# Attention on one core: another order of widths, decay sums, scores and chunk ends on TensorE

## The chip, the cores and the metric

The kernel runs on one core of a Trainium2 chip. The metric is the device time of one execution in microseconds (us); lower is better. The core has TensorE (PE, matrix products; PEld is its weight load), VectorE (DVE), ScalarE (ACT), GpSimd (POOL) and SyncE (SP, which issues transfers). Each works through its own instructions in the order in which they are written; semaphores tie the engines together.

## The reference

A block of a gated transformer on x of 32 batches x 512 rows x 512 columns: an mLSTM-like attention with 8 heads of 64 columns (queries from x, keys and values from a context), then a layer of experts, each row's choice of experts by a softmax. The attention part, cut to what matters:

```
gi = concat([q, k, v]);  ig = gi @ igate_w.T + igate_b;  fg = gi @ fgate_w.T + fgate_b
cs = cumsum(log_sigmoid(fg));  log_D = tril(cs_s - cs_t) + ig_t
D = exp(log_D - max(log_D));  C = (q @ k.T / sqrt(64)) * D
h = (C / (max(abs(C.sum(-1)), exp(-max_log_D)) + 1e-6)) @ v
x = x + tanh(g_xattn) * layernorm_per_head(h) * out_w
```

Then x = x + tanh(g_ffn) * experts(layernorm(x)).

## The kernel before

Two stages follow each other: `attention`, in a loop over batches, then `experts`, eight experts with four blocks of rows each. Only the first is touched.

**Attention, chunk by chunk.** A batch has 512 rows, cut into four chunks of 128 (TILES). Inside a chunk the products of queries and keys are formed and weighted with the decays; what lies before a chunk comes in by a running state. The eight heads go in four pairs (PAIRS), p = 0 to 3. For each pair TensorE has four steps: `decays(b, p)` sums the logarithms of the decays into the bank EX (10 products; ScalarE's `decay_factors` takes the exponential into C); `widths(b, p)` spreads a factor of each row over the columns of its heads (one product; VectorE's `weighted_queries` multiplies the queries with it); `scores(b, p)` is the product of queries and keys into the two banks QK (16 products; VectorE's `weighted_scores` multiplies them with C); `product(b, p)` applies the result to the values and the states, into A (ScalarE's `numerators` copies it out).

**The loop.** It has NB + 2 = 34 iterations i, and holds five batches at a time: b1 = i - 1 (its q and k are transposed and its gates worked out), b2 = i - 2 (the four pairs), b3 (end of pair 3, normalising), b5 = i - 5 (`turn_rows`, the transposes of its finished rows xfb for the router, and `logits`) and b6. `live(b)` says whether there is such a batch. Each engine's order in the loop is written out by hand.

**Gates.** For b1, `gates` (TensorE) sums the gate logits, `log_sigmoid` (ScalarE) takes their logarithms, `shift_gates` (TensorE) moves rows into the bank T1, `gate_runs` (VectorE) makes the running sums and `rise` out of it. `chunk_ends` (TensorE, two small products into T0) hands the ends of the chunks over to `gate_peaks` (VectorE), which copies them into `prior` and goes on to `peaks`. VectorE's order there is gate_runs(b1), weighted_queries(b2, 3), gate_peaks(b1), weighted_scores(b2, 3), inner_factors(b1) (which ends with `steps`). `peaks` is needed by decays(b1, 0), and `steps` by `turn_gates` (TensorE) at the end of the iteration.

**Banks.** T[0], T[1] and the two QK banks are shared by many short-lived products. The table in `iteration_fills` says which product goes to which of the four (the last number of an entry) and which engine empties it; `fill` makes TensorE wait until the bank's last content has been taken. By that table widths of pair 1 go to T0 and those of pairs 2 and 3 to T1. T1 holds the copy of q (column block 3) ahead of widths of pair 2, and the product of `shift_gates` ahead of widths of pair 3:

```
                    ("qw", b2, 2, "dve", 1), ("scores", b2, 2, None, None), ("shift", b1, 0, "dve", 1), ("qw", b2, 3, "dve", 1),
```

The first two `turn_rows` of b5 also go to T1 one after the other, and ScalarE empties them in `turned_rows`. ScalarE's order there is: copies of q and k (blocks 0 and 1 of b1), first_state(b2), second_norm(b5, (2, 3)) (which finishes xfb), squares(b3, 3), decay_factors(b2, 1), turned_rows(b5, 0), turned_rows(b5, 1). `scores` of pair 1 waits until VectorE has taken the states (S) out of the two QK banks.

Of the kernel before, what the change touches and what calls it, by code (L numbers as in the profile page):

```python
# [75 lines left out]
def spread(ap, axis, n):  # L76

    ap = ap.unsqueeze(axis)
    return ap.to_broadcast([n if i == axis else s for i, s in enumerate(ap.shape)])
# [9 lines left out]
def attention(nc, io, NB, dram, sm_all, tg, consts, stored, plan):  # L89
# [6 lines left out]
    with ExitStack() as ctx:  # L96
# [60 lines left out]
        def live(b):  # L157
            return 0 <= b < NB
# [36 lines left out]
        def fill(pe, kind, b, k):  # L195

            if ahead[kind, b, k]:
                pe.wait_ge(*ahead[kind, b, k])
            if (kind, b, k) in weighted:
                pe.wait_ge(*weighted[kind, b, k])  # L200
            return bank[kind, b, k]
# [46 lines left out]
        with nc.Block() as block:  # L248
# [410 lines left out]
            def _(pe):  # L659
# [8 lines left out]
                def turn(kind, b, c):  # L668

                    src, blocks = (q, None) if kind == "q" else (kraw, b % VBUF)  # L670
                    t = fill(pe, kind, b, c)
                    for j in range(TILES):
                        rows = q[:, j, :] if kind == "q" else kraw[:, b % VBUF, j, :]
                        mm = pe.transpose(t[:, j * P:(j + 1) * P], rows[:, c * P:(c + 1) * P], ident[:, :])
                    mm.then_inc(s["tfull"], 1)
# [62 lines left out]
                def scores(b, p):  # L738

                    g = PAIRS * b + p  # L740
                    if g:
                        pe.wait_ge(s["cc"], 2 * g)
                    for taken in cleared.get((b, p), ()):
                        pe.wait_ge(*taken)
                    for j in range(TILES):
                        jj = slice(j * P, (j + 1) * P)
                        for par in range(2):
                            r = slice(DH * par, DH * par + DH)
                            mm = pe.matmul(QK[:, par, jj], kT[r, b % 2, p, jj], qT[r, b % 2, p, jj], start=True, stop=True)  # L749
                    mm.then_inc(s["qk"], 1)  # L750

                def decays(b, p):

                    g = PAIRS * b + p
                    if g:
                        pe.wait_ge(s["dd"], g)
                    top, end = slice(0, DH), slice(DH, P)
                    for a, r, mask in ((0, top, (maskneg, maskswap)), (1, end, (maskswap, maskneg))):
                        for t, m in zip((top, end), mask):
                            pe.matmul(EX[t, a, :], identb[r, r], m[r, :], start=True, stop=False, skip_group_check=True)  # L760
                    if p == 0:
                        pe.wait_ge(s["rp"], b + 1)
                    for a, r in ((0, top), (1, end)):
                        ones_of = pick[r, p, :, :].rearrange("k a j -> k (a j)")
                        pe.matmul(EX[:, a, :], climb[r, b % 2, :], spread(ones_of, 2, P), start=False, stop=False, skip_group_check=True)
                    if p == 0:
                        pe.wait_ge(s["xm"], b + 1)
                    for par in range(2):
                        for a, r in ((0, top), (1, end)):
                            half = slice(a * 2 * P, (a + 1) * 2 * P)  # L770
                            mm = pe.matmul(EX[:, a, par * 2 * P:(par + 1) * 2 * P], sel[r, 2 * p + par, :], peaks[r, b % 2, half],
                                           start=False, stop=True, skip_group_check=True)
                            if par:
                                mm.then_inc(s["ee"], 1)

                def widths(b, p):

                    t = fill(pe, "qw", b, p)
                    pe.matmul(t[:, 0:SEQ - P], selP[:, 2 * p:2 * p + 2, :].rearrange("k a d -> k (a d)"), inner[:, b % 2, :], start=True, stop=True)\
                      .then_inc(s["tfull"], 1)  # L780
# [11 lines left out]
                def product(b, p):  # L792

                    g = PAIRS * b + p
                    pe.wait_ge(s["cc"], 2 * g + 2)
                    if p == 0:
                        wait_taken(pe, "st", b, TILES - 2)
                    wait_taken(pe, "qw", b, p)
                    if g:
                        pe.wait_ge(s["an"], g)  # L800
                    for j in range(TILES):
                        for par in range(2):
                            for a in range(2):
                                r = slice(DH * a, DH * a + DH)
                                mm = pe.matmul(A[r, par, j, 0:VW], C[:, 2 * (g % CRING) + par, j * P + DH * a:j * P + DH * a + DH],
                                               vc[:, b % 2, j, 2 * p + par, :], start=(j == 0), stop=(j == 0), skip_group_check=True)
                    for j in range(1, TILES):
                        for par in range(2):
                            r = slice(DH * par, DH * par + DH)
                            mm = pe.matmul(A[:, par, j, 0:VW], qw[r, g % 2, (j - 1) * P:j * P], S[r, j - 1, p, :],  # L810
                                           start=False, stop=True, skip_group_check=True)
                    mm.then_inc(s["af"], 1)

                for i in range(NB + 2):
                    b1, b2, b3, b5, b6 = i - 1, i - 2, i - 3, i - 5, i - 6

                    if live(b3):
                        product(b3, 3)
                    if live(b2):
                        widths(b2, 0)  # L820
                    if live(b1):
                        pe.wait_ge(s["q"], b1 + 1)
                        pe.wait_ge(s_cd[b1 % VBUF], 16 * (b1 // VBUF + 1))
                        for c in range(2):
                            turn("q", b1, c)
                            turn("k", b1, c)
                    if live(b2):
                        for j in range(TILES - 1):
                            chunk_state(b2, j)

                        decays(b2, 1)
                    if live(b5):
                        turn_rows(b5, 0)
                    if live(b2):
                        widths(b2, 1)
                        scores(b2, 1)
                    if live(b5):
                        turn_rows(b5, 1)
                    if live(b2):
                        product(b2, 0)  # L840
                    if live(b5):
                        turn_rows(b5, 2)
                    if live(b1):
                        turn("q", b1, 2)
                        turn("k", b1, 2)
                        turn("q", b1, 3)
                    if live(b6):
                        turn_logits(b6)
                    if live(b5):
                        turn_rows(b5, 3)  # L850
                    if live(b1):
                        turn("k", b1, 3)

                    if live(b2):
                        decays(b2, 2)
                        widths(b2, 2)
                        scores(b2, 2)
                    if live(b1):
                        gates(b1)
                    if live(b2):  # L860
                        product(b2, 1)
                    if live(b1):
                        if b1 == 0:
                            pe.wait_ge(s["prep1"], 1)
                        shift_gates(b1)

                    if live(b2):
                        decays(b2, 3)
                        widths(b2, 3)
                    if live(b1):  # L870
                        chunk_ends(b1)
                    if live(b2):
                        scores(b2, 3)
                    if live(b5):
                        logits(b5)
                    if live(b2):
                        product(b2, 2)
                    if live(b1):
                        decays(b1, 0)
                        scores(b1, 0)  # L880
                        turn_gates(b1)
# [971 lines left out]
```

## Time and profile before

| | us |
|---|---|
| median of 3 runs | 3052.46 |
| lowest, highest | 3051.99, 3055.52 |
| span of the profiled execution (first to last instruction) | 3051.6 |
| TensorE busy in it | 2948.7 (97%) |
| VectorE busy | 1819.7 (60%) |
| ScalarE busy | 1132.8 (37%) |
| GpSimd busy | 1065.5 (35%) |

The profiled execution's own time shown is its span; the median of the runs lies 0.9 us above it. The shares are means over two unlike stages: VectorE and ScalarE are far busier in attention than over the span. Instructions on TensorE are pipelined, so that one starts before the one ahead of it is over; where steps are added up, the distance from start to start is taken.

### The profile page before, as it was taken

What the parts mean: (1) busy time and instruction counts of PE and PEld (TensorE: products, weight loads), DVE (VectorE), ACT (ScalarE), POOL (GpSimd) and SP (SyncE); (2) the same over time, 40 slices, a digit from 0 to 9 for tenths busy, and PEclk for the clock granted to TensorE, in tenths of its full rate; (3) what the DMA queues carried; (4) which work ended last, traced back from release to release, by engine and by line L of the source; (5) the groups of instructions that cost most, each with busy time, mean ns of one, the idle gap of its engine ahead of it and who ended that gap; (6) DMA issues with size and microseconds to landing.
All of it is one profiled execution on the core that took longest, in us unless ns stands there. A gap on an engine that the chain in (4) does not pass through costs nothing.

```text
span 3051.6 us, 60802 instructions
## 1 busy us (share of the span) xinstructions
PE 2948.7 (97%) x24708; PEld 2395.3 (78%) x24708; DVE 1819.7 (60%) x5124; ACT 1132.8 (37%) x2025; POOL 1065.5 (35%) x1029
## 2 busy tenths in 40 slices
PE   6999999999997599999999999999999999999998
PEld 5888888888886477777777877787787787778886
DVE  6999999999998645354454444444434445444332
ACT  5788788787886211121121121122112122112110
POOL 4777777777776311111122111121112112121111
PEclk9999999999998699999999999999999999999999
DMA  3243444434443412241242132232123214222121
GB/s 122 100 160 120 162 139 149 161 123 165 141 134 113 131 40 37 35 99 31 46 99 48 36 80 35 37 96 62 31 38 93 41 31 111 38 50 57 35 37 24
DMA packets 140575, 250.71 MB, mean 82 GB/s; under 512 B 31968, under 2 KB 31968, under 8 KB 140296
## 3 DMA queue, kind: packets, MB, share of 16 engines
q1 hardware_dynamic: 106296, 170.80, 17.2%
q0 software_dynamic: 28672, 67.65, 12.6%
q10 hardware_dynamic: 5328, 8.36, 0.9%
q8 instruction: 197, 3.23, 0.4%
q14 instruction: 82, 0.67, 0.1%
HBM read 137.23 MB, written 101.19 MB: 78 GB/s over the span
## 4 chain that ended last, share of the span: by engine, by line
PE 64%; DVE 1%; DMA 1%; issue 0%; ACT 0%; POOL 0%; ACTq 0%; DVEq 0%; POOLq 0%
PE DN L1729 32%; PE UP L1700 30%; PE TT L1673 1%; DMA w_raw<-in_L_ffn_W_down 1%; DVE c_hit L1392 0%; PE c_bank L1385 0%; DVE down_lo L1258 0%; PE c_bank L1369 0%; DVE c_hit L1413 0%; ACT z L1643 0%; DVE c_within L1408 0%; ACT down_hi L1252 0%; POOL out_x L1618 0%; DVE c_gained L1445 0%; DVE mid_lo L1761 0%
## 5 line engine op out<-in xcount | busy, mean ns | idle before, releaser
L1618 POOL DMA_INDIRECT out_x<-y,slots x128 | 208.5, 1629 | 1621.1 <-DVE y L1785 1621.1
L1643 ACT ACTIVATE z<-UP,bup 128x512 f32<-128x512 f32 (+1 forms) x352 | 240.8, 686 | 1085.6 <-PE UP L1700 1066.5
L1729 PE MATMUL DN<-down_hi,mid_hi 128*128 128x512 f32 x1408 | 570.8, 405 | 0.0
L1700 PE MATMUL UP<-xT_hi,up_lo 128*128 128x512 f32 (+1 forms) x1408 | 555.5, 395 | 0.0
L1700 PE MATMUL UP<-xT_hi,up_hi 128*128 128x512 f32 (+1 forms) x1408 | 553.5, 393 | 1.8 <-DVE xT_lo L1740 0.9
L1700 PE MATMUL UP<-xT_lo,up_hi 128*128 128x512 f32 (+1 forms) x1408 | 552.0, 392 | 0.0
L1729 PE MATMUL DN<-down_hi,mid_lo 128*128 128x512 f32 x1280 | 505.8, 395 | 0.0
L1729 PE MATMUL DN<-down_lo,mid_hi 128*128 128x512 f32 x1280 | 505.7, 395 | 0.0
L1759 DVE CAST mid_hi<-z 128x512 fp32r<-128x512 f32 (+1 forms) x352 | 151.2, 429 | 486.4 <-ACT z L1643 486.4
L1783 DVE TENSOR_TENSOR y<-DN,bdn 128x512 f32<-128x512 f32 x128 | 88.5, 692 | 432.3 <-PE DN L1729 419.5
L1700 PEld LDWEIGHTS UP<-xT_hi,up_hi 128*128 128x128 f32 (+1 forms) x1408 | 260.3, 185 | 67.5 <-ACT z L1643 2.8
L1700 PEld LDWEIGHTS UP<-xT_lo,up_hi 128*128 128x128 f32 (+1 forms) x1408 | 259.8, 185 | 67.6 <-issue 0.5
L1700 PEld LDWEIGHTS UP<-xT_hi,up_lo 128*128 128x128 f32 (+1 forms) x1408 | 259.9, 185 | 65.5 <-issue 0.5
L1729 PEld LDWEIGHTS DN<-down_hi,mid_hi 128*128 128x128 f32 x1408 | 266.5, 189 | 56.1
L1729 PEld LDWEIGHTS DN<-down_hi,mid_lo 128*128 128x128 f32 x1280 | 240.4, 188 | 58.2
L1729 PEld LDWEIGHTS DN<-down_lo,mid_hi 128*128 128x128 f32 x1280 | 241.1, 188 | 50.1
L1761 DVE TENSOR_TENSOR mid_lo<-z,mid_hi 128x512 fp32r<-128x512 f32 (+1 forms) x352 | 244.1, 693 | 12.1
L1627 ACT ACTIVATE xT_hi<-TT 128x512 fp32r<-128x512 f32 x126 | 68.3, 596 | 467.0 <-PE TT L1673 446.9
L233 POOL TENSOR_TENSOR nsb<-nsb,rr 128x512 f32<-128x512 f32 x125 | 127.0, 1049 | 215.2 <-DVE nn L973 215.2
L1030 DVE SCALAR_TENSOR_TENSOR C<-QK,C 128x512 f32<-128x512 f32 x256 | 164.7, 685 | 8.5 <-PE QK L749 6.5
L749 PE MATMUL QK<-qT,kT 64*128 64x128 f32 x2048 | 146.4, 282 | 13.2 <-DVE S L1048 12.1
L1597 POOL DMA_INDIRECT xg<-rows_scratch,slots x128 | 137.5, 1075 | 56.3 <-issue 38.1
(264 smaller groups left out, 4971.9 us busy)
## 6 DMA issues: line engine op xcount, KB each, us to landing
xs<-in_x SPq DMA_DIRECT2D x64, 512.0 KB, 3.7
kraw<-in_ctx SPq DMA_DIRECT2D x32, 1024.0 KB, 7.3
out_x<-xs SPq DMA_DIRECT2D x32, 1024.0 KB, 12.5
rows_scratch<-xfb SPq DMA_DIRECT2D x32, 1024.0 KB, 10.6
w_raw<-in_L_ffn_W_down SPq DMA_DIRECT2D x40, 512.0 KB, 4.4
w_raw<-in_L_ffn_W_up SPq DMA_DIRECT2D x16, 682.5 KB, 4.1
mid_hi<-mid_hi ACTq DMA_DIRECT2D x32, 86.0 KB
mid_lo<-mid_hi ACTq DMA_DIRECT2D x32, 84.0 KB
```

The costliest lines, as they stand in the source:

```text
L233: ins = eng.tensor_tensor(n, n, spread(scale[:, j, :], 2, DH), ALU.mult)
L749: mm = pe.matmul(QK[:, par, jj], kT[r, b % 2, p, jj], qT[r, b % 2, p, jj], start=True, stop=True)
L1030: dve.scalar_tensor_tensor(out=c, in0=QK[:, par, :], scalar=DH ** -0.5, in1=c, op0=ALU.mult, op1=ALU.mult)\
L1597: pool.indirect_dma_start(xg[:, t, :], None, rows_v, bass.IndirectOffsetOnAxis(ap=slots[:, 4 * n + t:4 * n + t + 1], axis=0)).then_inc(s_r ...
L1618: pool.indirect_dma_start(out_rows, bass.IndirectOffsetOnAxis(ap=slots[:, m:m + 1], axis=0), y[:, t, :], None, compute_op=ALU.add).then_in ...
L1627: act.activation(xT[0][:, c, :], turned(n, c)[:, :], ACT.Copy).then_inc(s["thi"], 1)
L1643: act.activation(z[0:r, k % 2, :], UP[k % 3][0:r, :], ACT.Silu, bias=bup[0:r, e // 2, f:f + 1]).then_inc(s["z"], 1)
L1700: mm = pe.matmul(UP[k % 3][0:r, :], weights.up[wa][:, c, f * P:f * P + r], xT[xa][:, c, :], start=first, stop=(c == CH - 1 and wa == 1))
L1729: mm = pe.matmul(DN[m % 2][:, :], lhs, rhs, start=first, stop=(f == FCH - 1 and lhs is parts[-1][0]))
L1759: dve.tensor_copy(mid[0][0:r, f, :], z[0:r, k % 2, :]).then_inc(s["hi"], 1)
L1761: dve.tensor_tensor(mid[1][0:r, f, :], z[0:r, k % 2, :], mid[0][0:r, f, :].bitcast(FP32), ALU.subtract)\
L1783: dve.tensor_tensor(y[:, t, :], DN[m % 2][:, :], bdn[:, e % 2, :], ALU.add).then_inc(s["yp"], 1)
```

## The change

Only the order of calls in TensorE's loop changes; every product stays, with the same operands, banks and waits. In pair 1, `decays` moves from ahead of `turn_rows(b5, 0)` and `widths` to behind them, directly ahead of `scores`. In pair 2, `widths` and `decays` change places. In pair 3 they change places too, and `scores` follows `decays` directly; `chunk_ends(b1)`, which stood ahead of `scores`, comes behind. The other engines' orders stay as they are.

```
                         for j in range(TILES - 1):
                             chunk_state(b2, j)
 
-                        decays(b2, 1)
                     if live(b5):
                         turn_rows(b5, 0)
                     if live(b2):
                         widths(b2, 1)
+                        decays(b2, 1)
                         scores(b2, 1)
...
                     if live(b2):
+                        widths(b2, 2)
                         decays(b2, 2)
-                        widths(b2, 2)
                         scores(b2, 2)
...
                     if live(b2):
+                        widths(b2, 3)
                         decays(b2, 3)
-                        widths(b2, 3)
+                        scores(b2, 3)
                     if live(b1):
                         chunk_ends(b1)
-                    if live(b2):
-                        scores(b2, 3)
```

TensorE's order at pair 1, before, from behind the states' products to the scores. EX takes the decay sums, T1 the transposed rows (from xfb), T0 the widths (from inner), QK the scores; the brackets name the semaphores waited for (a_xf2: xfb is finished; a_ta and a_td: ScalarE or VectorE has emptied a bank; a_dd: an exponential has been taken; a_cc: scores have been weighted):

```order
L760 MATMUL EX<-maskneg,identb 64x512 [waits a_dd]
L760 MATMUL EX<-maskswap,identb 64x512 x2
L760 MATMUL EX<-maskneg,identb 64x512
L765 MATMUL EX<-pick,climb 128x512 x2
L771 MATMUL EX<-peaks,sel 128x256 x4
L683 MATMUL T1<-ident,xfb 128x128 [waits a_ta,a_xf2]
L683 MATMUL T1<-ident,xfb 128x128 x3
L779 MATMUL T0<-inner,selP 128x384 [waits a_ta]
L749 MATMUL QK<-qT,kT 128x128 [waits a_td,a_cc]
L749 MATMUL QK<-qT,kT 128x128 x7
```

The same stretch of TensorE's order after the change:

```order
L683 MATMUL T1<-ident,xfb 128x128 [waits a_ta,a_xf2]
L683 MATMUL T1<-ident,xfb 128x128 x3
L779 MATMUL T0<-inner,selP 128x384 [waits a_ta]
L760 MATMUL EX<-maskneg,identb 64x512 [waits a_dd]
L760 MATMUL EX<-maskswap,identb 64x512 x2
L760 MATMUL EX<-maskneg,identb 64x512
L765 MATMUL EX<-pick,climb 128x512 x2
L771 MATMUL EX<-peaks,sel 128x256 x4
L749 MATMUL QK<-qT,kT 128x128 [waits a_td,a_cc]
L749 MATMUL QK<-qT,kT 128x128 x7
```

The product that waits for xfb now comes directly behind the states' products, and the decay sums stand between the widths and the scores.

TensorE's order at pair 3, before, from the shift product to the scores. T1 takes the shift product and then the widths, T0 the two products of chunk_ends (a_xp and a_xt: VectorE's and ScalarE's part of `ends` is made; a_gs: the gate logits are there):

```order
L717 MATMUL T1<-gsum,shift 128x128 [waits a_gs,a_td]
L760 MATMUL EX<-maskneg,identb 64x512 [waits a_dd]
L760 MATMUL EX<-maskswap,identb 64x512 x2
L760 MATMUL EX<-maskneg,identb 64x512
L765 MATMUL EX<-pick,climb 128x512 x2
L771 MATMUL EX<-peaks,sel 128x256 x4
L779 MATMUL T1<-inner,selP 128x384 [waits a_td]
L724 MATMUL T0<-ends,later 128x8 [waits a_xt,a_xp]
L725 MATMUL T0<-unseen,ident 128x4
L749 MATMUL QK<-qT,kT 128x128 [waits a_cc]
L749 MATMUL QK<-qT,kT 128x128 x7
```

The same stretch of TensorE's order after the change:

```order
L717 MATMUL T1<-gsum,shift 128x128 [waits a_gs,a_td]
L779 MATMUL T1<-inner,selP 128x384 [waits a_td]
L760 MATMUL EX<-maskneg,identb 64x512 [waits a_dd]
L760 MATMUL EX<-maskswap,identb 64x512 x2
L760 MATMUL EX<-maskneg,identb 64x512
L765 MATMUL EX<-pick,climb 128x512 x2
L771 MATMUL EX<-peaks,sel 128x256 x4
L749 MATMUL QK<-qT,kT 128x128 [waits a_cc]
L749 MATMUL QK<-qT,kT 128x128 x7
L724 MATMUL T0<-ends,later 128x8 [waits a_xt,a_xp]
L725 MATMUL T0<-unseen,ident 128x4
```

Two products that use the bank T1 now follow each other directly, and the two products into T0 that VectorE reads next but one come last.

## Rows read from the trace of the kernel before

**Rows 1.** Windows: stretch; busy us of PE, PEld, DVE, ACT, POOL; clock, DMA, GB/s.

```profile
500.00:600.00 100.00, 98.52 (x1649) 83.83 (x1647) 93.72 (x263) 81.80 (x158) 77.56 (x79) 1.00 0.42 136
```

**Rows 2.** Waits of 150 to 900 us: waiter, releaser, us in total, times, longest.

```profile
PEld T L683 <- ACT xfb L510: 4.5, 26, 0.2
```

**Rows 3.** Timeline, TensorE, pair 1: start, duration, instruction, idle time before it.

```profile
508.47 0.40 PE L760 MATMUL EX<-maskneg,identb 64*64 64x512 bf16 x1
...
509.50 0.66 PE L683 MATMUL T<-ident,xfb 128*128 128x128 f32 x4
509.91 0.42 PE L779 MATMUL T<-inner,selP 128*128 128x384 f32 x1
510.69 1.16 PE L749 MATMUL QK<-qT,kT 64*128 64x128 f32 x16 [0.36 <-DVE S L1048]
511.79 0.66 PE L683 MATMUL T<-ident,xfb 128*128 128x128 f32 x4
```

**Rows 4.** Timeline, ScalarE, the same stretch: xfb, exponential of pair 1, first row copy.

```profile
507.94 1.51 ACT L510 ACTIVATE xfb<-xs,nn,rr 128x512 f32<-128x512 f32 x2
...
509.87 1.01 ACT L466 ACTIVATE C<-EX 128x1024 f32<-128x1024 f32 x1
510.78 0.59 ACT L457 ACTIVATE xfT<-T 128x512 f32<-128x512 f32 x1
```

**Rows 5.** Timeline, VectorE, the same stretch: the states.

```profile
508.80 1.75 DVE L1048 SCALAR_TENSOR_TENSOR S<-S,gb,QK 128x65 f32<-128x65 f32 x8
```

**Rows 6.** Timeline, TensorE, pair 2: decay sums and scores.

```profile
517.18 0.40 PE L760 MATMUL EX<-maskneg,identb 64*64 64x512 bf16 x1
...
518.54 1.16 PE L749 MATMUL QK<-qT,kT 64*128 64x128 f32 x16
```

**Rows 7.** Timeline, TensorE, pair 3 and the next batch's pair 0.

```profile
523.83 0.40 PE L760 MATMUL EX<-maskneg,identb 64*64 64x512 bf16 x1
...
524.82 0.44 PE L779 MATMUL T<-inner,selP 128*128 128x384 f32 x1
525.10 0.30 PE L724 MATMUL T<-ends,later 128*128 128x8 f32 x2
525.25 0.36 PE L725 MATMUL T<-unseen,ident 128*128 128x4 f32 x2
525.54 1.16 PE L749 MATMUL QK<-qT,kT 64*128 64x128 f32 x16
526.63 1.08 PE L692 MATMUL T<-xfT,Wr 128*32 128x128 f32 x32
...
529.54 0.40 PE L760 MATMUL EX<-maskneg,identb 64*64 64x512 bf16 x1
...
530.44 1.05 PE L749 MATMUL QK<-qT,kT 64*128 64x128 f32 x16
531.42 0.33 PE L733 MATMUL T<-ident,wt 128*128 128x128 f32 x1
```

**Rows 8.** Timeline, VectorE, the same stretch: rise, weighted queries, prior, weighted scores, steps.

```profile
524.00 0.29 DVE L1065 TENSOR_TENSOR rise<-T,cs 128x128 f32<-128x128 f32 x1 [0.29 <-PE T L717]
...
525.30 0.55 DVE L1039 SCALAR_TENSOR_TENSOR qw<-qT,T 128x384 f32<-128x384 f32 x1 [0.35 <-PE T L779]
525.77 0.15 DVE L1074 COPY prior<-T 128x4 f32<-128x4 f32 x1
...
528.59 1.29 DVE L1030 SCALAR_TENSOR_TENSOR C<-QK,C 128x512 f32<-128x512 f32 x2
...
531.08 0.17 DVE L1096 TENSOR_TENSOR steps<-spot,T 128x16 f32<-128x16 f32 x1
```

**Rows 9.** Timeline, ScalarE, pair 3: the exponential.

```profile
525.02 1.02 ACT L466 ACTIVATE C<-EX 128x1024 f32<-128x1024 f32 x1 [0.39 <-PE EX L771]
```

**Rows 10.** Timeline, TensorE, end of the stage: products behind long waits.

```profile
945.65 0.69 PE L788 MATMUL T<-uv,kraw 128*64 128x65 f32 x16 [1.04 <-DVE qw L1039]
...
977.30 1.12 PE L683 MATMUL T<-ident,xfb 128*128 128x128 f32 x4 [8.51 <-ACT xfT L457]
```

More of the change, by code:

```diff
@@ L829, in _ @@
                             chunk_state(b2, j)
-                        decays(b2, 1)
                     if live(b5):
@@ L835, in _ @@
                         widths(b2, 1)
+                        decays(b2, 1)
                         scores(b2, 1)
@@ L854, in _ @@
                     if live(b2):
+                        widths(b2, 2)
                         decays(b2, 2)
-                        widths(b2, 2)
                         scores(b2, 2)
@@ L867, in _ @@
                     if live(b2):
+                        widths(b2, 3)
                         decays(b2, 3)
-                        widths(b2, 3)
+                        scores(b2, 3)
                     if live(b1):
                         chunk_ends(b1)
-                    if live(b2):
-                        scores(b2, 3)
                     if live(b5):
```

## The prediction

> **What bounds the kernel now.** I read first which stage the edit lies in. Everything that moves stands in TensorE's loop of the attention stage, which runs to about 977 us of the span [rows 10]; the expert stage behind it is untouched and needs what attention leaves, so each microsecond lost or won in the loop goes through to the end. In a stretch in the middle of that stage TensorE is busy 98.52 us of 100, at the full granted clock, VectorE 93.72 and ScalarE 81.80 [rows 1]. TensorE sets the pace, but with VectorE and ScalarE so close that it can be made to wait by either. So I went on to the order of time inside one iteration and looked, at each of the three places of the edit, at what TensorE would wait for if the moved work were not there. The rows are of one iteration; the list of waits shows the same wait 26 times in 750 us [rows 2], which makes an iteration about 29 us.
>
> In that iteration TensorE stands still once, 0.36 us ahead of the scores of pair 1, until VectorE has emptied the score banks of the states (S, 508.80 + 1.75 = 510.55; the scores start at 510.69, so handing over from VectorE to TensorE takes 0.14) [rows 3, 5]. Ahead of that its weight load had waited only 0.17 us for ScalarE's xfb [rows 2]: that nearly invisible wait is what matters here.
>
> **Place 1: pair 1's decay sums move behind the first row transpose and the widths.** Before, the decay sums start at 508.47 and the row transpose at 509.50 [rows 3]. The transpose reads xfb, which ScalarE finishes at 507.94 + 1.51 = 509.45 [rows 4]; handing over takes 0.05. So the decay sums fill 1.03 us in which the transposes could not have run anyway. ScalarE cannot be earlier: it works back to back from the q and k copies, which follow TensorE's own transposes, so it moves along with TensorE. With the decay sums gone from there, TensorE waits 508.47 to 509.50. Then follow the widths 0.41 later (509.50 to 509.91 [rows 3]), the decay sums 0.28 behind them (a widths product to the next, 524.82 to 525.10 [rows 7]), the scores 0.90 behind those (529.54 to 530.44, the one place where they now stand so [rows 7]): 510.19 and 511.09. The wait for S (510.69) is swallowed. The scores are late by 0.40.
>
> There is a second step. ScalarE's exponential of pair 1 stands ahead of its two copies of transposed rows. It starts 1.19 us after the decay sums where it waits for them (523.83 to 525.02, idle 0.39 [rows 7, 9]), so at 511.38 instead of 509.87; the first copy comes 0.91 later (509.87 to 510.78) and takes 0.59 [rows 4]: done at 512.88. TensorE's second row transpose overwrites that copy's bank T1, so it can start at 512.93. TensorE would be there at 511.09 + 1.10 = 512.19 and waits 0.74 more. Before, that transpose started at 511.79 [rows 3]. Place 1 costs **1.14 us** an iteration. Bounds: 0.40 if the second wait were hidden, 1.50 if also the 0.36 for S came back.
>
> **Place 2: pair 2's widths ahead of its decay sums.** Now it is 1.36 us from decay sums to scores (517.18 to 518.54 [rows 6]); in the new order 0.28 + 0.90 = 1.18. The widths' bank T1 is emptied by ScalarE's copy of q, two copies ahead of the one that the scores wait for anyway, so I see no new wait. Gain **0.18 us**; bounds 0 (the scores also wait for the copy of k) and 0.18. The Trainium skill, "TensorE: Matmul & The Clock Gate", Part 3, says that a weight load overlaps running matmuls only where its row group differs; that would favour scores (half-height weights) behind decay sums over scores behind widths (full height), and the trace agrees with its 0.90 against 1.36. Without that effect this term is 0 and the sum below 77 us.
>
> **Place 3: pair 3's widths ahead of its decay sums, chunk_ends behind its scores.** The widths write bank T1 right after the shift product, and VectorE must have read that product: `rise`, 524.00 + 0.29 = 524.29 [rows 8]. Before, the decay sums ran meanwhile (523.83) [rows 7]. Now the widths wait until 524.29 + 0.14 = 524.43, the decay sums start at 524.71, the scores at 525.61 and chunk_ends at 526.71. TensorE's next work, the logits, starts 0.44 later (chunk_ends, 525.10 to 525.54) at 527.15 instead of 526.63: 0.52 late.
>
> What is queued behind chunk_ends is VectorE. Its `gate_peaks` is next but one after `rise`. VectorE wins the 0.35 that it now waits for the widths (525.30), so it is there at 525.42, but then stands before chunk_ends: the second product starts 0.15 after the first (525.10 to 525.25), takes 0.36, so it ends at 527.22; a VectorE operation starts 0.04 after a product's end (widths 524.82 + 0.44, then 525.30). So 527.26 instead of 525.77 [rows 7, 8]: VectorE is 1.49 late, and all behind it: the weighted scores of pair 3 (528.59 + 1.29 + 1.49 = 531.37) and `steps` (531.08 + 0.17 + 1.49 = 532.74).
>
> Does TensorE wait for those? The last decay sums of the next batch need `peaks`, which is out before the weighted scores begin; TensorE, 0.52 late itself, finds it done. The scores of the next batch's pair 0 overwrite the banks that the weighted scores read: 531.37 + 0.14 = 531.51, where TensorE arrives at 530.44 + 0.52 = 530.96. Wait 0.55. The gate transposes follow 0.98 later (530.44 to 531.42), at 532.49, and need `steps`: 532.88 instead of 531.42. Place 3 costs **1.46 us**. Lower bound 0.52 (TensorE's own delay, if VectorE caught up), upper 1.60 (the 1.49 plus a hand-over).
>
> After that TensorE is 1.46 late and VectorE 1.49: the next iteration starts from the same relative position, and since there is no idle time on TensorE that these could use up except the 0.36 already counted, the costs repeat.
>
> **The sum.** Place 1 needs the row transposes of batch b5 and the q and k copies of b1: iterations 5 to 32, 28 of them. Place 2 is in 32 iterations; chunk_ends with scores of pair 3 in iterations 2 to 32, 31 of them. 28 x 1.14 - 32 x 0.18 + 31 x 1.46 = 31.9 - 5.8 + 45.3 = 71.4 us. The profiled span is 3051.6, so 3123.0; the median is 0.9 above the span, so 3123.9, say **3124 us**. With all lower bounds 28 x 0.40 + 31 x 0.52 - 5.8 = 21.5 us (3074), with all upper ones 28 x 1.50 + 31 x 1.60 = 91.6 us (3144).
>
> **Rivals.**
> (a) *The two delays overlap.* If ScalarE reached xfb by its own pace and not by TensorE's, TensorE's 1.46 of place 3 would already have passed when it comes to place 1, and only the larger of the two would count: 31 x 1.46 - 5.8 = 39.5 us, 3092. For it: ScalarE is only 81.80% busy [rows 1]. Against it: ScalarE's work ahead of xfb follows TensorE's transposes one by one. 11%.
> (b) *Faster: the covers are not needed.* If xfb were ready at 508.47 and T1 free at 523.83, TensorE would save the wait for S (0.36 in 28 iterations) and 0.18 in each of three pairs in 32: 10.1 + 17.3 = 27.4 us, 3025. It decides itself at the row transpose: xfb would have to come about a microsecond earlier than 509.45, and VectorE's lateness at chunk_ends would have to stay off TensorE. Against it stand rows 2, 4 and 8. 5%.
> (c) *No change:* gain and a part of the delays cancel within 6 us, for which place 3 would have to cost nearly nothing. 4%.
> (d) *The clock falls with the new gaps.* At the half level four transposes take 1.12 us against 0.66 [rows 3, 10], a factor of 1.7; an iteration at that level would cost some 20 us more, three of them 60 (3184). But after 1.04 us of waiting the clock stayed full (the 16 products of the states, 0.69); it had fallen after 8.51 us [rows 10]. The new waits are each near 1 us. 3%.
>
> **How the numbers follow.** Forecast (both places cost about what is worked out): 77%, between 3105 and 3142. The range should hold the time 8 times in 10: from 3085, so that it takes in (a), to 3140, just under the upper bounds. Faster by over 0.2% (6 us, about what a measurement of this kernel can tell from no change): 5%; within: 4%; slower: 91%.
>
> **What would show it.** In the changed profile: TensorE idle about 1.03 us ahead of the first row transpose, released by ScalarE's xfb, and about 0.74 ahead of the second, released by ScalarE's xfT; no wait of the scores for S; TensorE idle 0.6 ahead of pair 3's widths, released by VectorE's `rise`; VectorE idle near 1.8 us ahead of the copy into `prior`, released by chunk_ends; TensorE idle about 0.55 ahead of pair 0's scores and 0.4 ahead of the gate transposes, both released by VectorE; an iteration some 2.4 us longer. It is wrong if the row transpose starts without a wait, if `prior` is not late, or if an iteration stays within 0.3 us of what it was.

## The result and the profile after

| | before | after |
|---|---|---|
| median, us | 3053.33 (4 runs) | 3124.59 (4 runs) |
| span of the profiled execution, us | 3051.6 | 3122.6 |
| ratio of the times | | 1.0227, 95% interval 1.0213 to 1.0241 |

The changed kernel is 71 us slower, as forecast (3124, range 3085 to 3140). The ratio is an estimate over all runs; the quotient of the two medians, 1.0233, lies in its interval. The first view of after is the same stretch of windows as in [rows 1], with the same columns:

```profile
500.00:600.00 100.00, 91.58 (x1568) 77.84 (x1568) 85.12 (x243) 75.42 (x145) 70.16 (x73) 1.00 0.40 132
```

TensorE is busy 91.58 us of 100 instead of 98.52, VectorE 85.12 instead of 93.72, and the clock is still full (1.00 of full speed): the same work is spread over more time. The list of waits between 150 and 900 us of after (waiter, releaser, us in total, times, longest) names where:

```profile
DVE prior L1073 <- PE T L725: 43.4, 24, 1.8
...
PE T L683 <- ACT xfb L510: 23.0, 24, 1.0
...
PE T L683 <- ACT xfT L457: 19.2, 24, 0.8
...
PE T L779 <- DVE rise L1064: 10.5, 24, 0.4
...
PE QK L749 <- DVE C L1029: 7.4, 24, 0.3
...
PE T L733 <- DVE steps L1095: 7.2, 24, 0.3
```

Each comes 24 times, once in an iteration. None of the six stands in the list of before with more than a fraction of this; where [rows 2] had 4.5 us in 26 waits of the weight load, TensorE itself now waits 23.0 us for xfb. The wait of pair 1's scores for S is gone.

The timeline of TensorE, after, shows place 1 (start, duration, instruction, idle time before it and its releaser); it answers to [rows 3]. The first line is the second row transpose of the iteration before:

```profile
519.24 0.66 PE L683 MATMUL T<-ident,xfb 128*128 128x128 f32 x4 [0.80 <-ACT xfT L457]
...
545.16 1.10 PE L788 MATMUL QK<-uv,kraw 128*64 128x65 f32 x32
547.22 0.66 PE L683 MATMUL T<-ident,xfb 128*128 128x128 f32 x4 [0.96 <-ACT xfb L510]
547.63 0.42 PE L779 MATMUL T<-inner,selP 128*128 128x384 f32 x1
547.98 0.40 PE L760 MATMUL EX<-maskneg,identb 64*64 64x512 bf16 x1
...
548.88 1.05 PE L749 MATMUL QK<-qT,kT 64*128 64x128 f32 x16
550.73 0.66 PE L683 MATMUL T<-ident,xfb 128*128 128x128 f32 x4 [0.80 <-ACT xfT L457]
```

Behind the states' products TensorE stands still 0.96 us until xfb is there, and 0.80 us more ahead of the second row transpose. Places 2 and 3 in TensorE's timeline, after (they answer to [rows 6, 7]):

```profile
524.07 0.63 PE L674 MATMUL QK<-ident,kraw 128*128 128x128 f32 x4
524.53 0.44 PE L779 MATMUL T<-inner,selP 128*128 128x384 f32 x1
524.91 0.40 PE L760 MATMUL EX<-maskneg,identb 64*64 64x512 bf16 x1
...
525.80 1.05 PE L749 MATMUL QK<-qT,kT 64*128 64x128 f32 x16
526.79 0.42 PE L709 MATMUL T<-qT,gW 128*32 128x128 f32 x8
...
530.57 0.49 PE L717 MATMUL T<-gsum,shift 128*128 128x128 f32 x2
531.50 0.44 PE L779 MATMUL T<-inner,selP 128*128 128x384 f32 x1 [0.44 <-DVE rise L1064]
...
532.77 1.06 PE L749 MATMUL QK<-qT,kT 64*128 64x128 f32 x16
533.76 0.39 PE L724 MATMUL T<-ends,later 128*128 128x8 f32 x2
534.00 0.36 PE L725 MATMUL T<-unseen,ident 128*128 128x4 f32 x2
534.29 1.08 PE L692 MATMUL T<-xfT,Wr 128*32 128x128 f32 x32
...
538.57 1.16 PE L749 MATMUL QK<-qT,kT 64*128 64x128 f32 x16 [0.30 <-DVE C L1029]
540.03 0.30 PE L733 MATMUL T<-ident,wt 128*128 128x128 f32 x1 [0.30 <-DVE steps L1095]
```

At place 2 the weight loads of the scores (PEld) stand as follows, first before, then after:

```profile
518.54 0.97 PEld L749 LDWEIGHTS QK<-qT,kT 64*128 64x128 f32 x16 [0.19 <-issue]
```

```profile
525.69 0.97 PEld L749 LDWEIGHTS QK<-qT,kT 64*128 64x128 f32 x16
```

Behind the widths (weights of full height, 128 rows) the first of them starts with the scores, at 518.54. Behind the decay sums (half height, 64 rows, like the scores) it starts 0.11 us ahead of the scores, at 525.69 for 525.80.

And VectorE's timeline there, after, which answers to [rows 8]:

```profile
531.15 0.29 DVE L1064 TENSOR_TENSOR rise<-T,cs 128x128 f32<-128x128 f32 x1 [0.29 <-PE T L717]
...
532.02 0.56 DVE L1038 SCALAR_TENSOR_TENSOR qw<-qT,T 128x384 f32<-128x384 f32 x1
534.40 0.16 DVE L1073 COPY prior<-T 128x4 f32<-128x4 f32 x1 [1.83 <-PE T L725]
```

VectorE no longer waits for the widths, and stands still 1.83 us for chunk_ends. To measure the places from start to start, five more rows of before are needed (TensorE's timeline, the iteration of [rows 3 to 9]): the states' products, the copy of k, the gates, the shift product, the second row transpose of the next iteration:

```profile
507.44 1.10 PE L788 MATMUL QK<-uv,kraw 128*64 128x65 f32 x32
...
516.62 0.63 PE L674 MATMUL QK<-ident,kraw 128*128 128x128 f32 x4
...
519.63 0.43 PE L709 MATMUL T<-qT,gW 128*32 128x128 f32 x8
...
523.41 0.49 PE L717 MATMUL T<-gsum,shift 128*128 128x128 f32 x2
...
540.94 0.66 PE L683 MATMUL T<-ident,xfb 128*128 128x128 f32 x4
```

| stretch of TensorE's order | before, us | after, us | difference | forecast |
|---|---|---|---|---|
| place 1: states' products to second row transpose | 511.79 - 507.44 = 4.35 | 550.73 - 545.16 = 5.57 | +1.22 | +1.14 |
| place 2: copy of k to gates | 519.63 - 516.62 = 3.01 | 526.79 - 524.07 = 2.72 | -0.29 | -0.18 |
| place 3: shift product to gate transposes | 531.42 - 523.41 = 8.01 | 540.03 - 530.57 = 9.46 | +1.45 | +1.46 |
| one iteration | 540.94 - 511.79 = 29.15 | 550.73 - 519.24 = 31.49 | +2.34 | +2.42 |

### The profile page after: what moved, and what is told of

Read it like the earlier page. It is cut to its first block, busy times and chain, and to the rows that moved or that the text cites. A ratio compares the mean times of both kernels' runs of the same rounds, so it can differ in the third digit from the quotient of the medians.

```text
span 3122.6 us, 60802 instructions
## 1 busy us (share of the span) xinstructions
PE 2949.3 (94%) x24708; PEld 2394.4 (77%) x24708; DVE 1817.7 (58%) x5124; ACT 1139.8 (37%) x2025; POOL 1065.2 (34%) x1029
## 4 chain that ended last, share of the span: by engine, by line
PE 62%; DVE 1%; DMA 1%; issue 0%; ACT 0%; POOL 0%; ACTq 0%; DVEq 0%; POOLq 0%
PE DN L1728 31%; PE UP L1699 30%; PE TT L1672 1%; DMA w_raw<-in_L_ffn_W_down 1%; DVE c_hit L1391 0%; PE c_bank L1384 0%; DVE down_lo L1257 0%; PE c_bank L1368 0%; DVE c_hit L1412 0%; ACT z L1642 0%; DVE c_within L1407 0%; POOL out_x L1617 0%; DVE c_gained L1444 0%; DVE mid_lo L1760 0%; ACT down_hi L1251 0%
## 5 line engine op out<-in xcount | busy, mean ns | idle before, releaser
L466 ACT ACTIVATE C<-EX 128x1024 f32<-128x1024 f32 x128 | 130.7, 1021 | 94.6 <-PE EX L771 91.1
```

The source lines that it names most:

```text
L466: act.activation(C[:, first:first + 2, :].rearrange("t r (a n) -> t r a n", a=2), EX[:, :, :].rearrange("t a (r n) -> t r a n", r=2), ACT. ...
```

## The experiments

All are compared with the kernel before, run on the same chip; differences are of medians, ratios have their 95% interval.

**Each place alone.** Place 1:

```
-                        decays(b2, 1)
                     if live(b5):
                         turn_rows(b5, 0)
                     if live(b2):
                         widths(b2, 1)
+                        decays(b2, 1)
                         scores(b2, 1)
```

> Only place 1 of the change: pair 1's decay sums behind the first row transpose and the widths; the rest is the kernel before. Theory (the two waits, for xfb and for the first row copy, cost 1.1 to 1.2 us in each of 28 iterations, and the costs of the places add up): 31 to 35 us slower than before. Rival (the delays of places 1 and 3 overlap, so that either place alone costs most of the whole): 45 us slower or more.

34.4 us slower (ratio 1.0112, 1.0097 to 1.0127). The theory holds and the rival falls. To take place 1 apart, ScalarE was also made to copy the first transposed rows ahead of pair 1's exponential:

```
                     if live(b3):
                         squares(b3, 3)
+                    if live(b5):
+                        turned_rows(b5, 0)
                     if live(b2):
                         decay_factors(b2, 1)
                     if live(b5):
-                        turned_rows(b5, 0)
                         turned_rows(b5, 1)
```

> Place 1 as in p1_only, and ScalarE takes the first row copy ahead of pair 1's exponential. Theory (of the 1.2 us some 0.75 is the second wait: the second row transpose waits for a copy that stands behind the exponential): that wait is gone, 0.4 to 0.5 us are left per iteration, 11 to 14 us slower than before. Rival (it is the late xfb and the late scores that cost, the second wait only shows them): 30 us or more, as p1_only.

11.0 us slower (1.0040, 1.0026 to 1.0054). The waits between 150 and 900 us of p1_only:

```profile
PE T L683 <- ACT xfb L510: 23.9, 25, 1.0
...
PE T L683 <- ACT xfT L457: 15.6, 25, 0.8
```

and of p1_copy_first, where the second has gone from TensorE's list altogether:

```profile
PE T L684 <- ACT xfb L510: 24.9, 26, 1.0
```

The wait for xfb is as long as ever, and costs 11 us: 0.4 us an iteration, since the 0.36 us for S and the quicker steps from decay sums to scores and from there to the second transpose come off it. The other two thirds of place 1, 23 us, are ScalarE's order: a copy that TensorE waits for stood behind an exponential that the move had made late.

Place 2:

```
                     if live(b2):
+                        widths(b2, 2)
                         decays(b2, 2)
-                        widths(b2, 2)
```

> Only place 2: pair 2's widths ahead of its decay sums; the rest is the kernel before. Theory (TensorE sets the pace, each 0.3 us less on it in 32 iterations goes through): 7 to 10 us faster than before, 3043 to 3046. Rival (VectorE runs back to back there, so TensorE only waits longer for S ahead of pair 1's scores): within 2 us of before.

2.6 us faster (0.9988, 0.9979 to 0.9997): short of the theory and just over the rival. Neither was the whole of it; see below. Place 3:

```
                     if live(b2):
+                        widths(b2, 3)
                         decays(b2, 3)
-                        widths(b2, 3)
+                        scores(b2, 3)
                     if live(b1):
                         chunk_ends(b1)
-                    if live(b2):
-                        scores(b2, 3)
```

> Only place 3: pair 3's widths ahead of its decay sums, scores behind them, chunk_ends last; the rest is the kernel before. Theory: 1.45 us in each of 31 iterations, 43 to 47 us slower than before. Rival (the delays of places 1 and 3 overlap): 60 us slower or more, nearly as much as the whole change.

50.5 us slower (1.0169, 1.0154 to 1.0185). That is over the theory's 47 and far from the rival's 60. A regular iteration of it (from one batch's states' products to the next's, as most iterations have it) is 30.63 us against 29.16, which is the 1.47 us of the theory. Its four runs lie in two pairs: 3100.78 (the profiled one) and 3101.10 are within a microsecond of the theory's upper end, 3106.23 and 3107.20 are 5 to 6 us longer. The excess is in these two, of which there is no trace; its cause is open.

**Place 3 in halves.** The widths alone ahead, chunk_ends as before:

```
+                        widths(b2, 3)
                         decays(b2, 3)
-                        widths(b2, 3)
                     if live(b1):
                         chunk_ends(b1)
```

> Half of place 3: pair 3's widths ahead of its decay sums, chunk_ends still ahead of the scores; the rest is the kernel before. Theory (the widths wait for rise and TensorE alone is late, by 0.55 us; VectorE, 0.43 us late at prior, is not waited for): 31 x 0.55 = 17 us slower than before. Rival (the widths' wait is the main cost of place 3): 35 us or more.

32.1 us slower (1.0107, 1.0092 to 1.0123), twice the theory. And chunk_ends alone behind the scores:

```
                         decays(b2, 3)
                         widths(b2, 3)
+                        scores(b2, 3)
                     if live(b1):
                         chunk_ends(b1)
-                    if live(b2):
-                        scores(b2, 3)
```

> The other half of place 3: decay sums and widths in the order of before, chunk_ends behind the scores. Theory (TensorE itself loses nearly nothing, but VectorE gets chunk_ends 1.06 us later, and TensorE then waits for it at pair 0's scores and at the gate transposes, 1.03 us in all): 31 x 1.03 = 32 us slower than before; with p3_widths more than p3_only, since there one delay hides a part of the other. Rival (VectorE's delay is taken up by its slack): within 5 us of before.

35.5 us slower (1.0115, 1.0100 to 1.0131), near the theory. From the shift product to the logits TensorE takes 515.36 - 511.95 = 3.41 us, with no wait, where it took 526.63 - 523.41 = 3.22 before:

```profile
511.95 0.49 PE L717 MATMUL T<-gsum,shift 128*128 128x128 f32 x2
...
515.36 1.08 PE L692 MATMUL T<-xfT,Wr 128*32 128x128 f32 x32
```

Its waits between 150 and 900 us:

```profile
DVE prior L1073 <- PE T L725: 26.9, 25, 1.1
...
PE QK L749 <- DVE C L1029: 7.7, 25, 0.3
PE T L733 <- DVE steps L1095: 7.6, 25, 0.3
```

So 0.19 us is TensorE's own; what sets the cost is that VectorE gets chunk_ends 1.1 us later and TensorE then waits for VectorE twice. The halves cost 67.6 us apart and 50.5 in one. One delay does hide a part of the other, but a smaller one than that: 13 of the 67.6 are a held multiplication on VectorE in p3_widths (below), which p3_only and p3_ends do not have (0.19 us in the mean in both). In regular iterations the halves without it cost 0.58 (p3_widths_wf, below) and 1.17 us, and 1.47 in one, so 0.28 us is hidden.

**What p2_only and p3_widths missed.** A timeline of VectorE and one of GpSimd in p3_widths, same moment:

```profile
394.97 0.68 DVE L942 TENSOR_TENSOR sm_all<-ex,sx 128x32 f32<-128x32 f32 x1
```

```profile
394.42 1.18 POOL L246 TENSOR_TENSOR xs<-xs,nsb 128x512 f32<-128x512 f32 x1
```

VectorE's small multiplication of the probabilities, two inputs from SBUF, takes 0.19 us when nothing is in its way. Here it takes 0.68 and ends at 395.65, 0.05 us after GpSimd's addition (394.42 + 1.18 = 395.60). In p2_only the same:

```profile
501.14 0.80 DVE L942 TENSOR_TENSOR sm_all<-ex,sx 128x32 f32<-128x32 f32 x1
```

```profile
500.72 1.18 POOL L246 TENSOR_TENSOR xs<-xs,nsb 128x512 f32<-128x512 f32 x1
```

It ends at 501.94, GpSimd at 501.90. So an order that moves VectorE against GpSimd by half a microsecond can put this multiplication behind an addition. That alone need not cost anything: in p1_only it is held in every iteration between 200 and 900 us (lines by group: count, busy us, mean ns, idle):

```profile
L942 DVE TENSOR_TENSOR sm_all<-ex,sx 128x32 f32<-128x32 f32 x23 | 16.8, 730 | 0.8
```

Yet no wait for S stands in p1_only's list, and its regular iteration is longer by the 1.2 us of place 1 alone (30.37 us against 29.16): TensorE waits for ScalarE there, and VectorE's lateness goes under in that. In p2_only and p3_widths no such wait stands ahead of the scores. The theory was then that VectorE's lateness reaches TensorE as a longer wait for S. It was tried by letting GpSimd weigh the values first; it then idles, waiting for VectorE's tm, while VectorE multiplies:

```
                         for j in range(TILES):
-                            if j == 1 and live(b1):
+                            if j == 0 and live(b1):
                                 weigh_v(b1)
```

> p3_widths with GpSimd's order of p2_wf. Theory (of the 32 us of p3_widths 0.5 us in each iteration is the held multiplication, seen as a wait for S of 0.75 instead of 0.37): the wait for S falls to 0.3 or less, 17 to 21 us slower than before. Rival (the widths' wait for rise alone costs all): 30 us or more.

19.2 us slower (1.0056, 1.0039 to 1.0073) instead of 32.1: the theory holds. The multiplication takes 0.19 us in the mean (0.61 in p3_widths), and the waits of the two kernels for S between 150 and 900 us, p3_widths first, are:

```profile
PE QK L749 <- DVE S L1048: 15.9, 24, 0.8
```

```profile
PE QK L749 <- DVE S L1048: 5.8, 23, 0.3
```

Of p3_widths' 32 us some 13 were the held multiplication. The other 19 are the new order on TensorE itself. In p3_widths_wf:

```profile
503.32 0.49 PE L717 MATMUL T<-gsum,shift 128*128 128x128 f32 x2
504.25 0.44 PE L779 MATMUL T<-inner,selP 128*128 128x384 f32 x1 [0.44 <-DVE rise L1065]
...
507.24 1.08 PE L692 MATMUL T<-xfT,Wr 128*32 128x128 f32 x32
```

From the shift product to the logits it takes 3.92 us instead of 3.22. Of the 0.70 more, 0.44 is the widths' wait for rise; the rest lies in steps without a wait. The shorter wait for S (0.25 us in a regular iteration, 0.37 before) gives 0.12 back.

> p2_only, and GpSimd weighs the values (uv) ahead of its first addition to xs instead of behind it; it then stands idle until VectorE's tm, while VectorE multiplies the probabilities (sm_all). Theory (in p2_only VectorE's multiplication of the probabilities, 0.19 us elsewhere, is held up to 1 us until GpSimd's addition ends, and VectorE's lateness there reaches TensorE as a longer wait for S): the multiplication takes 0.19 us in every iteration, iterations are even at 28.9 us or less, 6 to 10 us faster than before. Rival (place 2 gains nothing because VectorE is the bound there): as p2_only, 0 to 3 us faster than before.

7.4 us faster than before (0.9974, 0.9964 to 0.9983), the fastest kernel of this study, though its interval overlaps a little with that of p2_only. The lines by group between 200 and 900 us give the multiplication, in p2_only and in p2_wf:

```profile
L942 DVE TENSOR_TENSOR sm_all<-ex,sx 128x32 f32<-128x32 f32 x24 | 9.8, 408 | 0.8
```

```profile
L942 DVE TENSOR_TENSOR sm_all<-ex,sx 128x32 f32<-128x32 f32 x24 | 6.4, 265 | 0.8
```

It is not 0.19 in every iteration as expected: it still ends just behind GpSimd's last multiplication in most. But the long holds are gone, and with them most of the uneven iterations; a regular one is 28.96 us against 29.16 before, in p2_only and p2_wf alike. The trace of p2_only is of the longest of its 11 runs, so a usual run of it may have fewer long holds than its trace.

> The kernel before, with GpSimd's order of p2_wf. Theory: before, the multiplication is held in a few iterations only (0.26 us in the mean); 1 to 3 us faster than before, so that most of the gain of p2_wf is place 2's. Rival: the gain is GpSimd's order alone, as p2_wf.

No difference (1.0001, 0.9990 to 1.0011; the median 2.8 us above before, within the scatter of its runs). So the gain of p2_wf is not GpSimd's order by itself, as the rival had it. The theory's 1 to 3 us are not excluded by the interval, which reaches to 3 us faster, but nothing shows them. Most of the 7.4 us is place 2's; that GpSimd's order keeps it from being spent on held multiplications fits the two traces and is not shown further.

**A further attempt: pair 3's widths in the middle of its decay sums,** on top of place 2, between the climb products and the peak products, behind rise but, as planned, 0.33 us earlier for VectorE (decays takes a function that it calls there):

```
-                        decays(b2, 3)
-                        widths(b2, 3)
+                        decays(b2, 3, lambda: widths(b2, 3))
```

> Place 2 as in p2_only, and pair 3's widths between the mask and climb products and the peak products of its decay sums, that is 0.33 us earlier than before but still behind rise. Theory (VectorE waits 0.35 us for these widths; with them earlier it waits for chunk_ends instead, 0.1 us less in all): 2 to 4 us faster than p2_only. Rival (that wait of VectorE costs TensorE nothing): as p2_only.

4.4 us slower than before (1.0015, 1.0006 to 1.0024), 7 us worse than p2_only; neither theory nor rival had that. The multiplication is held no more than in p2_only (0.41 us in the mean in both).

> p2_split3 with GpSimd's order of p2_wf. Theory (what p2_split3 lost against p2_only was the held multiplication, and VectorE's shorter wait for the widths is worth little): as p2_wf or up to 3 us faster. Rival (the split itself costs TensorE 0.2 us in each iteration): 4 to 8 us slower than p2_wf.

1.1 us faster than before (0.9992, 0.9983 to 1.0002), but 6.3 us slower than p2_wf: the rival holds, the split itself costs. A regular iteration is 29.13 us against 28.96 in p2_wf. TensorE's timeline of p2_split3_wf:

```profile
492.04 0.49 PE L717 MATMUL T<-gsum,shift 128*128 128x128 f32 x2
...
493.22 0.44 PE L781 MATMUL T<-inner,selP 128*128 128x384 f32 x1
...
494.56 1.16 PE L749 MATMUL QK<-qT,kT 64*128 64x128 f32 x16
```

From the shift product to the scores it is 2.52 us, with the same products that took 525.54 - 523.41 = 2.13 before, and no wait for another engine: 0.39 us more with one full-height product put between half-height ones. The widths start 493.22 - 492.04 = 1.18 us behind the shift product, 524.82 - 523.41 = 1.41 before, so that VectorE gets them 0.23 us earlier, not 0.33. VectorE's earlier start gives about 0.2 of the 0.39 back (the wait for S is 0.25 us in a regular iteration, 0.47 in p2_wf).

## Why the prediction was right

The number was right to within 1 us, and each of the forecast waits stood where it was forecast. That it came so close is in part luck: place 1 was 0.08 us dearer an iteration than forecast and place 2 gave 0.11 more, 2.2 and 3.5 us in the sum, with opposite signs.

- *Place 1, first wait.* Forecast 1.03 us of idle time ahead of the row transpose, released by xfb; shown as 0.96. That its cover is worth only 0.4 us in the sum (forecast as the lower bound) is shown by p1_copy_first: 11.0 us, 28 x 0.4.
- *Place 1, second wait.* Forecast 0.74, shown as 0.80, and p1_copy_first takes it away alone: 23 us of 34. In all +1.22 for +1.14; most of the difference is the step from the widths to the decay sums, 547.98 - 547.63 = 0.35 us, which the forecast took from another pair of products as 0.28.
- *Place 2.* Forecast -0.18, which was also its upper bound; measured -0.29 in the changed kernel. The forecast's own term came out smaller: from widths to scores 525.80 - 524.53 = 1.27 us for the 1.36 of before, a gain of 0.09, since the decay sums follow the widths by 0.38 and not by 0.28. What it did not have is on either side: the widths follow the transposes of k sooner (524.07 to 524.53, 0.46) than the decay sums did (516.62 to 517.18, 0.56), and the gates follow the scores by 526.79 - 525.80 = 0.99 instead of 519.63 - 518.54 = 1.09. The 0.90 and 1.36 that the prediction sets side by side are not alike, since the 1.36 holds the widths too. The weight loads shown above agree with the row-group rule that the prediction cites from the Trainium skill ("TensorE: Matmul & The Clock Gate", Part 3): they run ahead behind half-height products and not behind a full-height one. p2_split3_wf prices the reverse of the change at 0.39 us. Alone, though, place 2 gives 0.20 us per iteration (28.96 against 29.16) and 2.6 us in all: with TensorE quicker, the wait for S grows (0.47 against 0.37) and VectorE's multiplication is held. The step "TensorE sets the pace" was thus true only of delays. A gain of 0.3 us on TensorE met VectorE, which the rows of before had shown with hardly any slack.
- *Place 3.* Forecast +1.46, measured +1.45, with VectorE at prior 1.83 us idle (1.8 forecast). TensorE's idle times are smaller than forecast: 0.44 ahead of the widths (0.6), 0.30 at pair 0's scores (0.55) and 0.30 at the gate transposes (0.4). The forecast had worked with distances between starts, and idle time is counted from the end of the product ahead; the distance from the shift product to the gate transposes is what it said. The halves show that both edits carry a cost of their own, and that they overlap by 0.28 us when made together.
- *The sum.* 28 x 1.22 - 32 x 0.29 + 31 x 1.45 = 69.9 us; the span grew by 71.0. The count of iterations and the additivity hold within the changed kernel. Of kernels with one place each it does not: 34.4 - 2.6 + 50.5 = 82.3 against 71.3. Some 7 of these 11 us are place 2, which brings 9 us (32 x 0.29) in the changed kernel and 2.6 alone; the other 4 are of the size of the excess in p3_only's two longer runs and are not explained.
- *Rivals.* (a), that the delays of places 1 and 3 overlap, is refuted: the whole costs 71 us and not 39.5, and TensorE's wait for xfb is 0.96 us an iteration with place 3 (23.0 us in 24) and without it (23.9 in 25 in p1_only). (b), faster, fell with the first wait, and (c), no change, with the cost of place 3. (d), the clock, did not move: 1.00 in the stretch.

## What to carry to other kernels

A wait that the trace shows as a fraction of a microsecond can be a long one that the work ahead of it covers: before moving work away from in front of an instruction, ask when its input is ready, not how long it waited. Of a small product that another engine stands behind, ask what that engine does next; here two tiny products moved behind 1.1 us of scores cost as much by themselves (35.5 us, p3_ends) as the whole of place 1 (34.4). And when the engine that sets the pace is made quicker, look at once at the next one and at what it shares: of place 2's gain 2.6 us were left alone, and 7.4 with GpSimd's order changed too.

## What the runs showed of the hardware

That a multiplication of 32 columns on VectorE is held for up to 1 us by a GpSimd addition I had not reckoned with: it shows not as idle time but as a longer instruction (0.68 and 0.80 us for 0.19 in the rows, 1.16 at the most in p2_only), ending 0.04 to 0.05 us after GpSimd's. The Trainium skill, "SBUF — State Buffer", Who interferes with whom, says that a VectorE instruction with two inputs in SBUF contends with a GpSimd instruction that reads SBUF, that the port pair which they share is an exclusive lock, and that the order of issue decides who blocks; the rows agree, in which GpSimd's addition starts first (394.42 and 394.97, 500.72 and 501.14). The other surprise is that one full-height product between half-height ones made TensorE 0.39 us slower over the same products (p2_split3_wf), more than the 0.28 us from that product's start to the next in [rows 7].
